# Batch 0's projection in two halves, gamma's tanh behind the spreads, and missed-row flags as one-element comparisons

## The reference

```
Q, K = h @ Wq.T, h @ Wk.T
sim = Q K^T / (sqrt(16) * 4)                    # 256 x 256 per batch, summed over 4 heads
threshold = 76th largest of each row            # k = int(256 * 0.3)
A = sigmoid(sim) * (sim >= threshold);  A = (A + A^T) / 2
x = x + (1 - sigmoid(gamma_raw)) * layernorm(x) + sigmoid(gamma_raw) * A
x = x + moe(layernorm(x))                       # 8 experts, top 2, 256 -> 256 -> 256 with gelu
```

## Time and profile before

| | us |
|---|---|
| median of 3 runs | 129.22 (128.85 to 129.48) |
| the profiled execution's own time | 129.01 |
| its span, first to last instruction | 127.2 |
| busy in the span: PE / DVE / ACT / POOL | 119.5 / 94.4 / 85.6 / 67.1 |
| mean granted TensorE clock | 0.999 |

### The profile page before, as it was taken

One profiled execution on the slowest core, in us unless ns is written; L12 is line 12 of the kernel. 1 busy time (PEld: TensorE's weight loads), 2 busy tenths in 40 slices (PEclk: granted clock), 3 DMA queues, 4 the chain that ended last, 5 costly groups with the idle time before them and its releaser, 6 DMA issues.

```text
span 127.2 us, 2759 instructions
## 1 busy us (share of the span) xinstructions
PE 119.5 (94%) x900; PEld 109.6 (86%) x900; DVE 94.4 (74%) x403; ACT 85.6 (67%) x210; POOL 67.1 (53%) x68
## 2 busy tenths in 40 slices
PE   6796898999899999999999999999999999999990
PEld 3453465899899999999999999999999999999990
DVE  0188899978956899999879899998866228523481
ACT  4189799899999877475967864957446554555500
POOL 2059937988659735650596256406952544444400
PEclk9999999999999999999999999999999999999999
DMA  1999999606998300020000000200000002000002
GB/s 53 205 368 417 406 376 160 130 5 88 207 173 125 75 0 3 0 88 0 3 3 0 5 0 3 82 3 5 0 0 0 5 0 82 0 0 8 0 0 82
DMA packets 3380, 10.05 MB, mean 79 GB/s; under 512 B 396, under 2 KB 868, under 8 KB 3364
## 3 DMA queue, kind: packets, MB, share of 16 engines
q1 hardware_dynamic: 2500, 6.71, 14.8%
q0 software_dynamic: 864, 3.15, 14.5%
HBM read 8.81 MB, written 1.05 MB: 77 GB/s over the span
## 4 chain that ended last, share of the span: by engine, by line
PE 74%; DVE 8%; ACT 6%; DMA 4%; POOL 3%; issue 2%; DVEq 0%; POOLq 0%
PE p_y L480 32%; PE p_h L458 32%; DMA w_lo<-w 4%; DVE acc L1070 2%; PE p_y L358 2%; ACT act_waste L546 1%; DVE top L893 1%; PE p_g L406 1%; PE p_a L382 1%; POOL w_lo L679 1%; POOL h_lo L700 1%; PE p_s L342 1%; PE p_a L335 1%; PE p_x L394 1%; ACT act_waste L539 1%
## 5 line engine op out<-in xcount | busy, mean ns | idle before, releaser
L700 POOL TENSOR_TENSOR h_lo<-h_act,h_hi 128x512 fp32r<-128x512 f32 x31 | 40.5, 1308 | 42.3 <-ACT h_hi L590 38.9
L582 ACT ACTIVATE h_act<-p_h,small_sb 128x256 f32<-128x256 f32 x64 | 26.6, 467 | 21.6 <-PE p_h L458 21.5
L458 PE MATMUL p_h<-xt_hi,w_hi 128*128 128x256 f32 x128 | 33.3, 282 | 0.5 <-DMA w_lo<-w 0.4
L458 PE MATMUL p_h<-xt_hi,w_lo 128*128 128x256 f32 x128 | 33.0, 279 | 0.0
L1070 DVE SCALAR_TENSOR_TENSOR acc<-p_y,comb,acc 128x256 f32<-128x256 f32 x55 | 24.0, 476 | 11.8 <-PE p_y L480 11.0
L480 PE MATMUL p_y<-w_hi,h_hi 128*128 128x256 f32 x126 | 26.0, 288 | 0.0
L458 PE MATMUL p_h<-xt_lo,w_hi 128*128 128x256 f32 x128 | 25.5, 280 | 0.0
L480 PE MATMUL p_y<-w_hi,h_lo 128*128 128x256 f32 x126 | 25.3, 282 | 0.0
L480 PE MATMUL p_y<-w_lo,h_hi 128*128 128x256 f32 x126 | 25.2, 282 | 0.0
L458 PEld LDWEIGHTS p_h<-xt_hi,w_hi 128*128 128x128 f32 x128 | 24.0, 188 | 1.3 <-DMA w_lo<-w 0.8
L458 PEld LDWEIGHTS p_h<-xt_hi,w_lo 128*128 128x128 f32 x128 | 24.0, 188 | 0.0
(11 more groups left out here) (141 smaller groups left out, 184.5 us busy)
## 6 DMA issues: line engine op xcount, KB each, us to landing
w_sb<-w SPq DMA_DIRECT2D x8, 512.0 KB, 8.2
w_lo<-w POOLq DMA_DIRECT2D x6, 512.0 KB, 5.6
x_sb<-x SPq DMA_DIRECT2D x1, 768.0 KB, 8.5
out<-acc SPq DMA_DIRECT2D x3, 256.0 KB, 2.5
x_sb<-x SPq DMA_DIRECT2D x1, 256.0 KB, 4.6
out<-acc SPq DMA_DIRECT2D x2, 128.0 KB, 2.0
attn_sb<-attn SPq DMA_DIRECT2D x1, 192.0 KB, 5.0
small_sb<-small SPq DMA_DIRECT2D x1, 97.5 KB, 4.4
```

Of the source, the lines that this page charges most:

```text
L458: last = nc.tensor.matmul(dst, w_[:, e, 0, k, c * P:(c + 1) * P], v[:, b % 2, k, :], start=n == 0, stop=n == len(trio) - 1)
L582: last = nc.scalar.activation(h_act[:, s % 2, c], tiled(p_h[s % 2])[:, c, :], ACT.Gelu, bias=b1_sb[:, e, c:c + 1])
L700: nc.gpsimd.tensor_tensor(h_lo[:, s % (LAG + 1)], h_act[:, s % 2], h_hi[:, s % (LAG + 1)], ALU.subtract).then_inc(h_lo_ready, 1)
```

## The change

Three edits. First, batch 0's `u` is no longer made by one matmul of 256 columns and one copy, but by two matmuls of 128 columns (into two PSUM banks) and two copies; the first `sim` tile waits for the first copy alone. Second, on ACT the tanh of gamma, and the wait for the DMA of the small constants, move behind `spread_of(0)`; on DVE the three operations on gamma (`gamma_terms`) and the four of `ln1_affine(0)` move behind both first guesses. Third, the flags: two DVE operations on 128x2 (`few`, then `missed` from `count` and `few`) become four on 128x1, a comparison each, with no operation that combines them; `missed` has four columns, and PE and the final reduce add all four. In each batch they stand between the two `drop_above` operations.

```diff
+            def u_of_tile(t):
+                nc.tensor.matmul(U_BANKS[t][0:D, 0:P], m_sb[:], ctx_sb[:, t * P:(t + 1) * P], start=True,
+                                 stop=True).then_inc(u_ready, 1)
...
             def sim_of(b):
-                pe.wait_ge(u_copied, b + 1)
-                for t in range(TILES):
+                for t in range(TILES):
+                    pe.wait_ge(u_copied, TILES + b if b else t + 1)
...
-                nc.tensor.matmul(p_a[0:1, 0:TILES], ones[:], missed[:], start=True, stop=True).then_inc(missed_sum, 1)
+                nc.tensor.matmul(p_a[0:1, 0:2 * TILES], ones[:], missed[:], start=True, stop=True).then_inc(missed_sum, 1)
...
-            u_copy(0)
+            for t in range(TILES):
+                u_copy_tile(t)
+            sim_copy(0)
+            spread_of(0)
             act.wait_ge(small_in, 16)
             nc.scalar.activation(gam[:, 0:1], gamma_sb, ACT.Tanh, scale=0.5).then_inc(gam_th, 1)
-            sim_copy(0)
-            spread_of(0)
...
-                dve.wait_ge(few_ready, b + 1)
-                nc.vector.scalar_tensor_tensor(missed[:], count[:], TOP_K, few[:], ALU.is_ge,
-                                               ALU.add).then_inc(missed_ready, 1)
+                for t in range(TILES):
+                    dve.wait_ge(counted, b * TILES + t + 1)
+                    nc.vector.tensor_scalar(missed[:, 2 * t:2 * t + 1], count[:, t:t + 1], TOP_K - WINDOW, None,
+                                            ALU.is_lt)
+                    last = nc.vector.tensor_scalar(missed[:, 2 * t + 1:2 * t + 2], count[:, t:t + 1], TOP_K, None,
+                                                   ALU.is_ge)
+                last.then_inc(missed_ready, 1)
...
                     step_of_tile(nc.vector.scalar_tensor_tensor(left[:, t], above[:, t], REPLACED, sim_of_tile(b, t),
                                                                 ALU.mult, ALU.add))
-                flag_missed(b)
+                    if t == 0:
+                        flag_missed(b)
...
             ln1(0)
-            gamma_terms()
             for t in range(1, TILES):
                 sim_copy(t)
             for t in range(TILES):
                 mean(0, t)
-            first_guess(0, 0)
+            for t in range(TILES):
+                first_guess(0, t)
+            gamma_terms()
             ln1_affine(0)
-            for t in range(1, TILES):
-                first_guess(0, t)
```

More of the change, by code:

```diff
@@ L133, in xattn_moe_program @@
         count = sb("count", [P, TILES])
-        few = sb("few", [P, TILES])
-        missed = sb("missed", [P, TILES])
+        missed = sb("missed", [P, 2 * TILES])
         ones = sb("ones", [P, 1])
@@ L238, in xattn_moe_program @@
         better_ready = sem("better_ready")
-        few_ready = sem("few_ready")
         b2_added = sem("b2_added")
@@ L348, in sum_missed @@
                 if b == 0:
-                    pe.wait_ge(u_copied, 1)
+                    pe.wait_ge(u_copied, TILES)
                     pe.wait_ge(const_set, 2)
@@ L366, in similarities @@
                 pe.wait_ge(m_copied, 1)
-                u_of(0)
+                for t in range(TILES):
+                    u_of_tile(t)
                 sim_of(0)
@@ L485, in _ @@
             similarities()
-            pe.wait_ge(u_copied, BATCHES)
+            pe.wait_ge(u_copied, TILES + BATCHES - 1)
             transpose_masked(0)
@@ L514, in _, with u_copy_tile @@
         def _(act):
+            def u_copy_tile(t):
+                act.wait_ge(u_ready, t + 1)
+                nc.scalar.activation(u_sb[:, t * P:(t + 1) * P], U_BANKS[t][0:D, 0:P], ACT.Copy,
+                                     scale=SIM_SCALE).then_inc(u_copied, 1)
             def u_copy(b):
-                act.wait_ge(u_ready, b + 1)
+                act.wait_ge(u_ready, TILES + b)
                 nc.scalar.activation(u_sb[:, b * N:(b + 1) * N], U_BANKS[b][0:D, 0:N], ACT.Copy,
@@ L851, in count_above @@
                                         accum_out=count[:, t:t + 1]).then_inc(counted, 1)
-            def flag_few(b):
-                dve.wait_ge(counted, (b + 1) * TILES)
-                nc.vector.tensor_scalar(few[:], count[:], TOP_K - WINDOW, None, ALU.is_lt).then_inc(few_ready, 1)
             def flag_missed(b):
@@ L882, in drop_above @@
                     dve.wait_ge(counted, b * TILES + t + 1)
-                    if t == TILES - 1:
-                        if b == 0:
-                            flag_few(b)
                     step_of_tile(nc.vector.scalar_tensor_tensor(left[:, t], above[:, t], REPLACED, sim_of_tile(b, t),
                                                                 ALU.mult, ALU.add))
-                flag_missed(b)
+                    if t == 0:
+                        flag_missed(b)
             def take_eight(r):
@@ L910, in know_missed @@
                 dve.wait_ge(missed_sum, b + 1)
-                nc.vector.tensor_reduce(any_missed[:, b:b + 1], p_a[0:1, 0:TILES], AX.X, ALU.add).then_inc(
+                nc.vector.tensor_reduce(any_missed[:, b:b + 1], p_a[0:1, 0:2 * TILES], AX.X, ALU.add).then_inc(
                     missed_known, 1)
@@ L1131, in _ @@
                         count_above(nxt, t)
-                    flag_few(nxt)
                     drop_above(nxt)
```

## The result

| | median us | executions | ratio to before, 95% interval |
|---|---|---|---|
| before | 129.22 (128.85 to 129.54) | 5 | |
| changed | 127.97 (127.79 to 128.64) | 5 | 0.989 (0.985 to 0.993) |

In each of the three later groups of runs the kernel before has a median of 129.4 (26 to 33 executions each), and the changed kernel, run again in the first of them, has 128.02, with a ratio of 0.987 (0.983 to 0.992): 1.37 us faster. All medians leave out slow executions, which here are two of before's 28 in that group (148.59 us at a granted clock of 0.79, and 130.99 us).

The account below looks back on a forecast made before the run. PE's full stretch from 33.8 us was taken as the bound, with only its start movable. Halves and gamma gave 0.05 us, flags most of the rest, capped at 0.65; sum 0.62, so 129.22 - 0.62 = 128.6 us, range 128.25 to 129.1.

Parts of the forecast that it names:

- What bounds: PE is busy from 33.8 us; the change can only move that start, set by the DMA for expert 4.
- The cap: ACT's queue is free for `xt_hi` at 22.15 instead of 22.80, so at most 0.65 us get through.
- Edit 1 and 2: Batch 0's path: halves gain 0.53 us at sim, spent on DVE by seven small operations before the middle guess.
- The term of 0.05: Net gain of halving u and moving gamma's work: 0.05 us, from -0.05 to 0.53.
- Edit 3: Batch 0's flags: no longer held by POOL's casts, MAX8 starts at 13.18 instead of 13.85, gaining 0.60 to 0.75 us.
- The term of 0.57: The new flags' share of the 0.62 us forecast gain, without the 0.05 from halves and gamma's move.
- A: One-element flag comparisons are held by POOL's casts as `few` was, MAX8 0.50 us later: 129.7 us; chance 0.06.
- B: Path gains, but expert 4's DMA queues behind others and lands as before, PE waits longer: 129.2 us; chance 0.08.
- C: `choose` on DVE is held by POOL's DMA issue until 16.4, losing 0.5 us: 129.05; with other partial losses, chance 0.14.
- D: Expert 0's weights land earlier or ACT's queue is shorter, cap 0.8 or more: 128.4 us or less; chance 0.08.
- The range: Forecast time from 128.25 to 129.1 us, with 0.3 us either way for the runs' scatter.

Follow-up runs that it names:

- after_again: The changed kernel run again unchanged, for a second trace: median 128.02 us against 129.39 before; the traced execution took 128.18 us.
- after_3: The changed kernel run once more unchanged, for a third trace: the traced execution took 128.08 us.
- gamma_early: The full change, but with gamma's tanh, terms and affine factors left where they stood before: 127.62 us, ratio 0.986 to before.
- flags_only: The kernel before with only the new one-element flag comparisons, unused buffer `few` kept: 128.49 us, ratio 0.992 to before.
- kernels with pinned casts: A POOL wait for DVE's count added ahead of two casts: before 128.96 us (first tile's count) or 129.53 (second tile's), changed kernel 128.31 (second tile's).
- two_element: The full change with each flag comparison done once on 128x2, not twice on 128x1: 129.01 us, 0.99 above the full change.

## Why the prediction was right and where it was wrong

**What bounds: one step of this failed.** Right is that PE's full stretch begins with the DMA for expert 4, issued at 27.55 (forecast 27.5), `up(4)` at 33.22 (33.2). Wrong is "The change takes no work from PE there. So it can only move the point at which that stretch begins." That put the stretch itself at nothing. It got shorter: 80.54 us instead of 80.90 from `up(7)` to the last add, 0.36 us, in every trace. What of the change does it is open.

**The cap:** right in kind, and its size hit by luck. ACT is the last to arrive in the first trace of the changed kernel by 0.05 us, in after_again it arrives together with the transposes, and in after_3 it idles 0.29. I had read ACT's queue as running without a gap from 13.95 to 22.15. It has a hidden wait of 0.13 us. ACT and DVE before, then ACT in after_again:

```profile
20.07 1.08 ACT L560 ACTIVATE w_hi<-w_sb 128x1024 fp32r<-128x1024 f32 x1
21.15 0.51 ACT L539 ACTIVATE act_waste<-sim,neg_guess 128x256 f32<-128x256 f32 x1
...
20.90 0.34 DVE L820 TENSOR_SCALAR neg_guess<-spread,neg_mean 128x1 f32<-128x1 f32 x2
```

```profile
20.22 1.08 ACT L569 ACTIVATE w_hi<-w_sb 128x1024 fp32r<-128x1024 f32 x1
21.17 0.53 ACT L548 ACTIVATE act_waste<-sim,neg_guess 128x256 f32<-128x256 f32 x1
```

The signs start 1.08 us behind the weight step before, right behind DVE's guess, and 0.95 in the changed kernel. So before's cap was 0.78 and not 0.65. In after_again the queue is 0.14 shorter and starts 0.15 later (14.10), and so 22.17 meets my 22.15. What I also left out is that the cap is no constant: it hangs on the landing of expert 0's weights, 7.9 to 9.1 in the traces.

**Edit 1 and 2:** the working was right (sim 5.04, middle guess 9.37 against 9.41; only the second spread came at 7.61, 0.11 earlier than I had), and so was the finding that edit 2 spends on DVE what edit 1 gains; gamma_early shows it, and with it that 0.40 us were left lying. The term of 0.05 measured 0.11 at MAX8 and at `up(0)`. By the medians the full change is 0.47 below flags_only; the other 0.36 is PE's stretch.

**Edit 3: this step failed in size.** Mechanism and place were right: the flags were held by POOL's casts, one-element comparisons are not. I took the hold from one execution, in which `few` and `missed` cost 1.10 us together, and wrote a gain at MAX8 of 0.60 to 0.75 as if it were a property of the kernel. It depends on where the flags fall in POOL's row of operations, and so on a DMA: 0.94 us together at a first cast at 8.43, 2.05 at 8.03. The kernel before has executions of both kinds, from 128.6 to 130.5; my trace, 129.01, was of the cheap kind. And where the hold is long the cap is loose, since both follow the same landing in opposite directions: at 8.07 in flags_only ACT was free for `xt_hi` at 21.70, so that 1.46 us got through. The term of 0.57 (0.62 less the 0.05 of edits 1 and 2) measured 0.90 by the medians.

So the 1.37 us between the medians are 0.90 from the flags, 0.11 from edits 1 and 2 on the path, and 0.36 from PE's stretch. That they add up to the hundredth is luck, with medians of 6 to 26 executions. The first is shown by flags_only and by the kernels with pinned casts, the second by traces, and the third is seen in every trace and not explained. The excess over the forecast of 0.62 is nearly half and half the flags (0.33) and PE's stretch (0.36).

**The rivals.** A (comparisons held) is out: 0.15 us each under a cast, in every trace. B (the DMA lands when it did) is out: issue and landing both moved. C (`choose` in POOL's DMA issue) is out: at 15.75 and 15.89 it took 0.22 and 0.23 us beside the issue that starts at 15.48, as it did without one. D, more gain, is what happened, with a chance of 0.08. Its two reasons, an earlier landing and a shorter queue of ACT, both have something to them, but the gain comes from the dear flags that go with an early landing, and from PE's stretch, and neither was named.

**The range** had 0.3 us for the runs' scatter. The scatter of the runs shown, 0.63 us over three, was a hint at a wait of varying length, but no proof: the changed kernel, whose flags are never held, scatters by 0.85 over its five.

## What to carry to other kernels

Where an operation's duration is set by what another engine happens to be doing, one trace gives one draw of it: take the hold from both sides, the shortest and the longest that the other engine's neighbouring operations allow, and ask what event sets the phase. If that event is a DMA's landing, removing the hold gains more in the median than in a trace of a cheap execution, and it narrows the spread. A bottleneck that the change doesn't touch is still worth timing from one fixed step to another, before and after: some 0.01 us in a group of twelve matmuls can't be seen in a table of busy times and made a quarter of this gain. And an operation moved off one engine's idle time onto another's path must be paid where it lands: the three edits together were slower than two of them.

## What the runs showed of the hardware that I had not expected

A `TENSOR_SCALAR` on 128x2 fp32 that meets a running GpSimd cast takes up to 1.07 us (two_element), while the same operation on 128x1 takes 0.15. The landing of the same DMA, with the same issues ahead of it, differs by up to 1.2 us between executions (first cast at 7.93 in gamma_early, 9.14 in the first trace of the change). PE's full stretch runs at one of two paces, 80.9 or 80.5 us for the same work at a granted clock of 1.00, by the kernel and not by the execution. And PE's four transposes before `xt_hi` start 0.11 to 0.15 us apart in some executions and 0.21 to 0.24 in others: in after_3 the time from `xn` to `xt_hi` is 1.47 us, in after_again 1.24. The granted clock of these stretches reads 1.00 in both; what makes them slower stays open.
